# Attention over 128 blocks: the order of SyncE's waits ahead of the keys' transpose, and of the third unit's scores and maxima products

## The chip, the cores and the metric

The kernel runs on one core of a Trainium2 chip. The metric is the time of one execution on the device in microseconds (us), as the median of several runs. The core has TensorE (matrix products), VectorE, ScalarE, GpSimd and SyncE, each with its own queue of instructions, and 16 DMA engines. Engines meet at semaphores only: an instruction waits until a semaphore has reached a count, and all behind it on its queue wait with it.

## The reference

An audio tower of three stages over x of 128 blocks, 256 time steps, 192 channels: a tokenizer that turns 256 steps into 127 tokens, an attention with eight heads, and a feed-forward stage that picks one of four experts by token. The change is in the attention. Cut to it:

```python
def _L0_attn_ref(x, w_qkv, w_proj, b_proj):
    ...
    hd = C // H
    g = hd // 3
    scale = hd ** (-0.5)
    qkv = (x @ w_qkv.T).reshape(B, N, 3, H, hd).transpose(2, 0, 3, 1, 4)
    q, k, v = (qkv[0], qkv[1], qkv[2])
    q3, q4, q5 = (q[..., :g], q[..., g:2 * g], q[..., 2 * g:])
    k3, k4, k5 = (k[..., :g], k[..., g:2 * g], k[..., 2 * g:])
    v3, v4, v5 = (v[..., :g], v[..., g:2 * g], v[..., 2 * g:])
    ...
    x3 = merge(_attn(q4, jnp.concatenate([k3, k4], axis=2), jnp.concatenate([v3, v4], axis=2), scale))
    x4 = merge(_attn(q5, jnp.concatenate([k3, k5], axis=2), jnp.concatenate([v3, v5], axis=2), scale))
    x5 = merge(_attn(q5, jnp.concatenate([k4, k5], axis=2), jnp.concatenate([v4, v5], axis=2), scale))
    out = jnp.concatenate([x3, x4, x5], axis=2)
    return out @ w_proj.T + b_proj

h = h + _L0_attn_ref(_layernorm(h, axis=-1), L0_attn_w_qkv, L0_attn_w_proj, L0_attn_b_proj)
```

B is 128 blocks, N 127 tokens, C 192, H 8 heads of 24 channels, g 8.

## The kernel before

Four stages follow one another: `tokenize`, `norm_terms` (the layer norm's terms of all blocks), `attend`, and, after terms again, `feed_forward`. Only `attend` is touched.

`attend` is a pipeline over the 128 blocks, written out by hand. Each engine has a function `body(i, r)` that is run for i from -4 to 130 (r = i mod 4 picks ring buffers); the middle iterations stand in a hardware loop of four bodies, so that one pass of the loop is four blocks and ends with a branch. In iteration i, different engines work at different blocks:

- GpSimd normalises block i + 4 into `hx` (L818 to L826), splits `raw` into fp16 halves: the keys of block i + 3 (L801, L804, signal `pool_k`), its queries (L807, L810, signal `pool_q`; L812, signal `pool_q5`), and splits the finished `att` (L833, L835, signal `pool_y`).
- SyncE issues five DMA transposes between buffers of the core, each of which TensorE needs as an operand: `xt` of block i + 3 (L534), keys `kt` (L539) and queries `qt` (L544) of block i + 2, `yt` of block i - 2 (L549) and `qm`, the queries with their maxima in them, of block i + 1 (L555). Its helper `ready(signal, count)` waits for a signal and then raises a semaphore of SyncE's own (L527); where the count depends on the loop's register, a register instruction (L526) stands in the queue as well.
- TensorE runs `products(i, r, u)` for the four units u = 0 to 3, called first to fourth unit here. A unit makes the scores of two heads of block i (L583, `qm` by `kt`): `p_s1` in two halves, `p_s5` in two, `p_s0` in two; and, of a later block, the products of which VectorE takes the maxima (L587, `qt` by `kt`): two into `p_maxa` and two into `p_maxb`. The first two units work at the maxima products of block i + 1, the last two at those of block i + 2, so the third unit (u = 2) is the first that needs a block's `kt` and `qt` (semaphores `dma_k`, `dma_q`). All these matmuls use 24 or 32 of the array's 128 rows, named by j in the code: b, c, d, a are rows of four different groups, and `fourth` and `fifth` share theirs with c and d. Between the units stand the outputs (L653, probabilities by values), behind the third one qkv's product of block i + 3 (L620 to L626, into `p_z`) and a transpose (L664), behind the fourth the projection (L620 to L626 again, into `p_z`).
- ScalarE takes exponentials of the units' scores, L696 of `p_s1`, L700 of `p_s5`, L703 of `p_s0`; behind those of the third unit it copies qkv's product to `raw` (L721) and `vn` (L722).
- VectorE takes the maxima, L746 of `p_maxa` (signals `dve_ma`), L750 of `p_maxb` (`dve_mb`); behind the second unit's it puts the minima of two into the queries (L766, L767, signal `dve_min`).

`qt` has two buffers. Before SyncE writes one, it waits for the second unit's maxima products of the block that used it, `pe_ma[1]` and `pe_mb[1]`, which TensorE raises one iteration earlier. `kt` has four; before writing one it waits for the fourth unit's scores of block i - 2, `pe_s0[3]`.

Of the kernel before, what the change touches and what calls it, by code (L numbers as in the profile page):

```python
# [30 lines left out]
def seen(count):  # L31

    return max(count, 0) if isinstance(count, int) else count


def within(x, n):

    return not isinstance(x, int) or 0 <= x < n
# [412 lines left out]
def attend(nc, t, NB):  # L451

    with ExitStack() as ctx:
# [3 lines left out]
        U = 4  # L457
        NQ, NK = 3 * HEADS, 3 * HEADS
        K0 = NQ * 32
# [8 lines left out]
        qk = sb("qk", [128, 2, K0 + NK * 32], F16)  # L468
        vn = sb("vn", [128, U, 3 * HEADS * 32])
        kt = sb("kt", [128, U, 3, GRP, 128], F16)  # L470
# [8 lines left out]
        p_ma = ps("p_maxa", [128, 8, 128])  # L479
        p_mb = ps("p_maxb", [128, 4, 128])  # L480
        p_s = [ps("p_s0", [128, 4, 128]), ps("p_s1", [128, 4, 128])]
        p_s5 = ps("p_s5", [128, 4, 128])
# [10 lines left out]
        pool_khigh, pool_k, pool_qhigh, pool_q, pool_q5 = (sem(n) for n in ("pool_khigh", "pool_k", "pool_qhigh", "pool_q", "pool_q5"))  # L493
        dma_x, dma_k, dma_q, dma_y, dma_qm = (sem(n) for n in ("dma_x", "dma_k", "dma_q", "dma_y", "dma_qm"))
        pe_qkv, act_qk, act_v = sem("pe_qkv"), sem("act_qk"), sem("act_v")
        pe_ma = [sem(f"pe_ma{u}") for u in range(4)]
        pe_mb = [sem(f"pe_mb{u}") for u in range(4)]
        dve_ma = [sem(f"dve_ma{u}") for u in range(4)]
        dve_mb = [sem(f"dve_mb{u}") for u in range(4)]
        dve_min = sem("dve_min")  # L500
        pe_half = [sem(f"pe_half{u}") for u in range(4)]
        pe_s1 = [sem(f"pe_s1{u}") for u in range(4)]
        pe_s0 = [sem(f"pe_s0{u}") for u in range(4)]
        act_e5, act_e1, act_e0 = ([sem(f"act_e{n}{u}") for u in range(4)] for n in (5, 1, 0))
# [5 lines left out]
        def loop(eng, body):  # L510

            for i in range(-4, 3):
                body(i, i % U)
            rounds = (NB - 7) // U
            with eng.Fori(0, rounds) as j:
                for r in range(U):
                    body(j * U + (3 + r), (3 + r) % U)
            for i in range(3 + U * rounds, NB + 3):
                body(i, i % U)

        @block.sync
        def _(sp):

            def ready(signal, count):

                sp.wait_ge(signal, count)  # L526
                sp.sem_inc(sp_ready, 1)  # L527

            def body(i, r):
                if within(i + 3, NB):  # L530
                    ready(pool_x, seen(i + 4))
                    if within(i + 2, NB):
                        ready(pe_qkv, seen(i + 3))
                    sp.dma_start_transpose(xt[:, :, :], hx[:, (r + 1) % 2, :]).then_inc(dma_x, 16)  # L534
                if within(i + 2, NB):
                    ready(pool_k, seen(i + 3))
                    if within(i - 2, NB):
                        ready(pe_s0[3], seen(i - 1))
                    sp.dma_start_transpose(kt[:, (r + 2) % U].rearrange("p k g n -> p (k g) n"), qk[:, r % 2, K0:K0 + 768]).then_inc(dma_k, 16)  # L539
                    ready(pool_q, seen(i + 3))  # L540
                    if within(i, NB):
                        ready(pe_ma[1], seen(2 * (i + 1)))
                        ready(pe_mb[1], seen(i + 1))
                    sp.dma_start_transpose(qt[:, r % 2].rearrange("p k g n -> p (k g) n"), qk[:, r % 2, 0:512]).then_inc(dma_q, 16)  # L544
                if within(i - 2, NB):
                    ready(pool_y, seen(i - 1))
                    if within(i - 3, NB):
                        ready(pe_proj, seen(i - 2))
                    sp.dma_start_transpose(yt[:, :, :], ay[:, :]).then_inc(dma_y, 16)  # L549
                if within(i + 1, NB):  # L550
                    ready(dve_min, seen(i + 2))
                    ready(pool_q5, seen(i + 2))
                    if within(i - 1, NB):
                        ready(pe_s0[3], seen(i))
                    sp.dma_start_transpose(qm[:, (r + 1) % 2].rearrange("p v g n -> p (v g) n"), qk[:, (r + 1) % 2, 0:768]).then_inc(dma_qm, 16)  # L555
            loop(sp, body)

        def z_reader(i, use):
# [10 lines left out]
        def _(pe):  # L569
# [3 lines left out]
            def products(i, r, u):  # L573

                g, lo = u // 2, 2 * (u % 2)
                ahead, gm = (1, 1) if u < 2 else (2, 0)
                bm, rk, rq = i + ahead, (r + ahead) % U, (r + ahead) % 2
                a, b, c, d = lo, lo + 1, 2 - lo, 3 - lo
                fourth, fifth = (c, d) if u < 2 else (d, c)
                has_s, has_m = within(i, NB), within(bm, NB)  # L580

                def score(o, j, kind, versions, half=g):
                    return nc.tensor.matmul(o, kt[full(j), r, kind, half, :], qm[full(j), r % 2, versions, half, :],  # L583
                                            start=True, stop=True, skip_group_check=True)

                def maximum(o, j, kind, cols, half=gm):
                    return nc.tensor.matmul(o, qt[short(j), rq, kind, half, :], kt[short(j), rk, cols, half, :],  # L587
                                            start=True, stop=True, skip_group_check=True)

                if has_s:  # L590
                    if u == 0:
                        pe.wait_ge(dma_qm, seen(16 * (i + 1)))
                    pe.wait_ge(act_e1[u - 1] if u else act_e1[3], seen(i + 1 if u else i))
                    score(p_s[1][:, 0:2, :], b, 0, slice(0, 2))
                if has_m:
                    if u == 2:
                        pe.wait_ge(dma_k, seen(16 * (bm + 1)))
                        pe.wait_ge(dma_q, seen(16 * (bm + 1)))
                    pe.wait_ge(dve_ma[u - 1], seen(i + 2 if u < 3 else i + 3))
                    maximum(p_ma[:, 0:3, :], c, 1, slice(0, 3)).then_inc(pe_ma[u], 1)  # L600
                    maximum(p_ma[:, 4:7, :], d, 1, slice(0, 3)).then_inc(pe_ma[u], 1)
                if has_s:
                    score(p_s[1][:, 2:4, :], b, 1, slice(0, 3, 2)).then_inc(pe_s1[u], 1)
                if has_s:
                    pe.wait_ge(act_e5[u - 1] if u else act_e5[3], seen(i + 1 if u else i))
                    score(p_s5[:, 0:2, :], fifth, 2, slice(1, 3), 0)
                    score(p_s5[:, 2:4, :], fifth, 2, slice(1, 3), 1).then_inc(pe_half[u], 1)
                if has_s:
                    pe.wait_ge(act_e0[u - 1] if u else act_e0[3], seen(i + 1 if u else i))
                    score(p_s[0][:, 0:2, :], a, 0, slice(0, 2))  # L610
                    score(p_s[0][:, 2:4, :], a, 1, slice(0, 3, 2)).then_inc(pe_s0[u], 1)
                if has_m:
                    pe.wait_ge(dve_mb[u - 1], seen(i + 2 if u < 3 else i + 3))
                    maximum(p_mb[:, 0:2, :], fourth, 0, slice(0, 2), 0)
                    maximum(p_mb[:, 2:4, :], fourth, 0, slice(0, 2), 1).then_inc(pe_mb[u], 1)
# [51 lines left out]
            def body(i, r):  # L667
                before = (r - 1) % U
                if isinstance(i, int) and i == -2:
                    pe.wait_ge(consts, 3)  # L670

                products(i, r, 0)
                outputs(i - 1, before, 0, 2)
                outputs(i - 1, before, 1, 0)

                products(i, r, 1)
                outputs(i - 1, before, 1, 1)
                outputs(i - 1, before, 1, 2)

                products(i, r, 2)  # L680
                qkv(i)
                outputs_t(i)

                products(i, r, 3)
                proj(i)
                outputs(i, r, 0, 0)
                outputs(i, r, 0, 1)
# [522 lines left out]
```

## Time and profile before

| | us |
|---|---|
| median of 3 runs | 1877.03 (1873.08 to 1880.6) |
| the profiled execution | 1871.97 |
| its span, first to last instruction | 1870.2 |

| engine | busy us | share of the span |
|---|---|---|
| TensorE, matmuls | 1749.2 | 94% |
| TensorE, weight loads (beside matmuls) | 1016.4 | 54% |
| VectorE | 1498.9 | 80% |
| ScalarE | 1444.0 | 77% |
| GpSimd | 1251.8 | 67% |

Busy time is the time in which an engine has an instruction under way. Matmuls overlap each other, so a TensorE that is shown busy isn't at its peak. In a timeline a line is one instruction, or several of one source line in a row (x4), from the first start to the last end; "idle before" in brackets is the time in which the engine had nothing under way and what ended it, "issue" if nothing that the profile shows did. Waits of a queue itself, SyncE's signals and TensorE's semaphore instructions among them, have no lines of their own there and are seen as gaps. The attention stage runs from about 345 to 1400 us of the span.

### The profile page before, as it was taken

The numbers are of one execution on the slowest core, as the hardware profiler recorded it, in microseconds if no ns is written. First come the engines' busy times: TensorE is split into PE (matmuls) and PEld (weight loads), VectorE is DVE, ScalarE is ACT, GpSimd is POOL, SyncE is SP. The second block draws the span as 40 slices with busy tenths as digits, with TensorE's granted clock in tenths as the row PEclk, the third lists the DMA queues.
The fourth block names the chain that finished last, engine by engine and source line by source line (L and its number), as shares of the span: only waits on it lengthen the run. The fifth ranks groups of instructions, "written<-read, shape, count | busy, mean of one in ns | idle before, by whom it ended". The sixth has DMA issues, their size and how long they took to land. (4 is left out here: it accounts for less than half of the span.)

```text
span 1870.2 us, 56704 instructions
## 1 busy us (share of the span) xinstructions
PE 1749.2 (94%) x19008; PEld 1016.4 (54%) x19008; DVE 1498.9 (80%) x3546; ACT 1444.0 (77%) x2983; POOL 1251.8 (67%) x2306
## 2 busy tenths in 40 slices
PE   5999999589999999999999999999994999999999
PEld 3677777144444444444444444444442777777776
DVE  6877778589999999999999999999984555555554
ACT  4666666288888888888888888888884777777775
POOL 5777776477777777777777777777753565656661
PEclk9999999599999999999999999999997999999999
DMA  7344442154444444444444444444441333333332
GB/s 192 95 111 111 111 111 67 39 83 89 86 90 89 89 87 90 89 89 87 89 90 88 89 89 90 88 89 89 89 76 28 71 69 69 70 67 70 67 74 54
DMA packets 503935, 159.49 MB, mean 85 GB/s; under 512 B 452176, under 2 KB 503120, under 8 KB 503888
## 3 DMA queue, kind: packets, MB, share of 16 engines
q1 hardware_dynamic: 503888, 158.90, 40.1%
q8 instruction: 26, 0.43, 0.1%
q14 instruction: 21, 0.17, 0.0%
HBM read 37.26 MB, written 12.48 MB: 27 GB/s over the span
## 5 line engine op out<-in xcount | busy, mean ns | idle before, releaser
L746 DVE TENSOR_REDUCE tops<-p_maxa 128x6 f32<-128x762 f32 x512 | 483.7, 945 | 50.5 <-PE p_maxa L587 38.9
L653 PE MATMUL p_o<-probs,vn 127*32 127x256 f32 x6144 | 410.7, 385 | 0.4 <-DVE att L776 0.4
L696 ACT ACTIVATE probs<-p_s 128x512 f32<-128x512 f32 x512 | 306.3, 598 | 126.6 <-PE p_s L583 126.3
L583 PE MATMUL p_s<-qm,kt 32*128 32x256 f16 x3072 | 369.9, 272 | 3.3
L750 DVE TENSOR_REDUCE tops<-p_maxb 128x4 f32<-128x508 f32 x512 | 346.6, 677 | 0.0
L703 ACT ACTIVATE probs<-p_s 128x512 f32<-128x512 f32 x512 | 310.9, 607 | 0.0
L700 ACT ACTIVATE probs<-p_s 128x512 f32<-128x512 f32 x512 | 304.0, 594 | 0.0
L1055 DVE TENSOR_TENSOR gel_lo<-gel,gel_hi 128x512 f16<-128x512 f32 x192 | 151.2, 788 | 168.1 <-ACT gel_hi L1027 168.1
L583 PEld LDWEIGHTS p_s<-qm,kt 32*128 32x128 f16 x3072 | 149.3, 92 | 229.3 <-issue 126.4
L801 POOL TENSOR_TENSOR qk<-raw,one 128x384 f16<-128x384 f32 x128 | 105.7, 826 | 228.2 <-ACT raw L721 228.2
L653 PEld LDWEIGHTS p_o<-probs,vn 127*32 127x32 f32 x6144 | 160.5, 109 | 140.6 <-issue 74.4
L1019 ACT ACTIVATE gel<-f_w,b 128x512 f32<-128x512 f32 x192 | 131.9, 687 | 117.4 <-PE f_w L968 117.4
L587 PE MATMUL p_maxa<-kt,qt 24*128 24x384 f16 x1024 | 173.4, 333 | 37.3 <-issue 18.8
L587 PE MATMUL p_maxb<-kt,qt 24*128 24x256 f16 x1024 | 196.5, 272 | 0.2
L979 PE MATMUL f_y<-w_hi,gel_hi 128*128 128x192 f16 x768 | 188.8, 246 | 0.2 <-DVE gel_lo L1055 0.2
L981 PE MATMUL f_y<-w_hi,gel_lo 128*128 128x192 f16 x768 | 188.9, 246 | 0.0
L980 PE MATMUL f_y<-w_lo,gel_hi 128*128 128x192 f16 x768 | 188.8, 246 | 0.0
L1125 POOL TENSOR_TENSOR f_hx<-f_hn,f_one 128x192 f16<-128x192 f32 x120 | 85.5, 712 | 153.7 <-ACT f_hn L1006 151.0
L208 ACT ACTIVATE tanhs<-pa 128x384 f32<-128x384 f32 x128 | 62.7, 490 | 99.2 <-PE pa L154 99.2
L1027 ACT ACTIVATE gel_hi<-gel 128x512 f16<-128x512 f32 x192 | 120.9, 630 | 7.0
L396 POOL TENSOR_TENSOR diag<-ident,weight 128x256 f32<-128x256 f32 x128 | 79.2, 620 | 54.1 <-DVE weight L296 44.9
L183 PE MATMUL ph<-zs,band 128*128 128x192 f32 x512 | 105.4, 330 | 3.1 <-DVE band L317 2.2
(212 smaller groups left out, 4509.9 us busy)
## 6 DMA issues: line engine op xcount, KB each, us to landing
xt_a<-in_xt SPq DMA_DIRECT2D x32, 512.0 KB, 4.4
xt_b<-in_xt SPq DMA_DIRECT2D x64, 256.0 KB, 5.1
out<-out_sb SPq DMA_DIRECT2D x32, 336.0 KB, 2.6
xt<-hx SPq DMA_TRANSPOSE x128, 2.4
kt<-qk SPq DMA_TRANSPOSE x128, 2.8
qt<-qk SPq DMA_TRANSPOSE x128, 2.4
qm<-qk SPq DMA_TRANSPOSE x128, 2.7
yt<-ay SPq DMA_TRANSPOSE x128, 2.3
```

What stands on the lines that cost most here:

```text
L583: return nc.tensor.matmul(o, kt[full(j), r, kind, half, :], qm[full(j), r % 2, versions, half, :], start=True, stop=True, skip_group_check ...
L587: return nc.tensor.matmul(o, qt[short(j), rq, kind, half, :], kt[short(j), rk, cols, half, :], start=True, stop=True, skip_group_check=True)
L653: last = nc.tensor.matmul(p_o[32 * j:32 * j + 32, blocks, :], vn[0:NP, r, src:src + 32], probs[0:NP, r % 2, QUAD * g + j, kind * 256:(kind ...
L696: nc.scalar.activation(probs[:, r % 2, h + 1, 0:512], p_s[1][:, :, :].rearrange("p x n -> p (x n)"), ACT.Exp, scale=SCALE).then_inc(act_e1 ...
L700: nc.scalar.activation(probs[:, r % 2, fifth:HEADS:QUAD, 512:768], p_s5[:, :, :].rearrange("p (h x) n -> p h (x n)", h=2), ACT.Exp, scale= ...
L703: nc.scalar.activation(probs[:, r % 2, h, 0:512], p_s[0][:, :, :].rearrange("p x n -> p (x n)"), ACT.Exp, scale=SCALE).then_inc(act_e0[u], 1)
L746: nc.vector.tensor_reduce(top[:, q, 6 * pair:6 * pair + 6].rearrange("p (e k) -> p e k", e=2), p_ma[:, :, :].rearrange("p (e k) n -> p e k ...
L750: nc.vector.tensor_reduce(top[:, q, 24 + 4 * fourth:28 + 4 * fourth], p_mb[:, :, 0:NP], AX.X, ALU.max, negate=True)\
L979: nc.tensor.matmul(o, ghi[:, c % 3, n], t.w2_hi[:, c, :], start=False, stop=False)
L980: nc.tensor.matmul(o, ghi[:, c % 3, n], t.w2_lo[:, c, :], start=False, stop=False)
L981: last = nc.tensor.matmul(o, glo[:, c % 3, n], t.w2_hi[:, c, :], start=False, stop=(c == HCH - 1))
L1055: nc.vector.tensor_tensor(glo[:, c % 3, :], gel[:, c % 2, :], ghi[:, c % 3, :], ALU.subtract).then_inc(dve_lo[c], 1)
```

## The change

SyncE: in the part of its body for block i + 2, the waits `pe_ma[1]`, `pe_mb[1]` (which stood between `kt`'s and `qt`'s transposes) and `pe_s0[3]` (which stood between the wait for `pool_k` and `kt`'s transpose) now stand ahead of the wait for `pool_k`. TensorE: two pieces of a unit become functions, `large` (the wait for `kt` and `qt` and the two products into `p_maxa`) and `odd` (the second half of `p_s1` and both of `p_s5`); the units 0, 1 and 3 run them in the order they had, the third unit runs `odd` first.

```diff
--- before.py
+++ after.py
@@ -533,14 +533,14 @@
                         ready(pe_qkv, seen(i + 3))
                     sp.dma_start_transpose(xt[:, :, :], hx[:, (r + 1) % 2, :]).then_inc(dma_x, 16)
                 if within(i + 2, NB):
-                    ready(pool_k, seen(i + 3))
-                    if within(i - 2, NB):
-                        ready(pe_s0[3], seen(i - 1))
-                    sp.dma_start_transpose(kt[:, (r + 2) % U].rearrange("p k g n -> p (k g) n"), qk[:, r % 2, K0:K0 + 768]).then_inc(dma_k, 16)
-                    ready(pool_q, seen(i + 3))
                     if within(i, NB):
                         ready(pe_ma[1], seen(2 * (i + 1)))
                         ready(pe_mb[1], seen(i + 1))
+                    if within(i - 2, NB):
+                        ready(pe_s0[3], seen(i - 1))
+                    ready(pool_k, seen(i + 3))
+                    sp.dma_start_transpose(kt[:, (r + 2) % U].rearrange("p k g n -> p (k g) n"), qk[:, r % 2, K0:K0 + 768]).then_inc(dma_k, 16)
+                    ready(pool_q, seen(i + 3))
                     sp.dma_start_transpose(qt[:, r % 2].rearrange("p k g n -> p (k g) n"), qk[:, r % 2, 0:512]).then_inc(dma_q, 16)
                 if within(i - 2, NB):
                     ready(pool_y, seen(i - 1))
@@ -587,24 +587,35 @@
                     return nc.tensor.matmul(o, qt[short(j), rq, kind, half, :], kt[short(j), rk, cols, half, :],
                                             start=True, stop=True, skip_group_check=True)
 
+                def large(do):
+
+                    if do:
+                        if u == 2:
+                            pe.wait_ge(dma_k, seen(16 * (bm + 1)))
+                            pe.wait_ge(dma_q, seen(16 * (bm + 1)))
+                        pe.wait_ge(dve_ma[u - 1], seen(i + 2 if u < 3 else i + 3))
+                        maximum(p_ma[:, 0:3, :], c, 1, slice(0, 3)).then_inc(pe_ma[u], 1)
+                        maximum(p_ma[:, 4:7, :], d, 1, slice(0, 3)).then_inc(pe_ma[u], 1)
+
+                def odd(do):
+
+                    if do:
+                        score(p_s[1][:, 2:4, :], b, 1, slice(0, 3, 2)).then_inc(pe_s1[u], 1)
+                        pe.wait_ge(act_e5[u - 1] if u else act_e5[3], seen(i + 1 if u else i))
+                        score(p_s5[:, 0:2, :], fifth, 2, slice(1, 3), 0)
+                        score(p_s5[:, 2:4, :], fifth, 2, slice(1, 3), 1).then_inc(pe_half[u], 1)
+
                 if has_s:
                     if u == 0:
                         pe.wait_ge(dma_qm, seen(16 * (i + 1)))
                     pe.wait_ge(act_e1[u - 1] if u else act_e1[3], seen(i + 1 if u else i))
                     score(p_s[1][:, 0:2, :], b, 0, slice(0, 2))
-                if has_m:
-                    if u == 2:
-                        pe.wait_ge(dma_k, seen(16 * (bm + 1)))
-                        pe.wait_ge(dma_q, seen(16 * (bm + 1)))
-                    pe.wait_ge(dve_ma[u - 1], seen(i + 2 if u < 3 else i + 3))
-                    maximum(p_ma[:, 0:3, :], c, 1, slice(0, 3)).then_inc(pe_ma[u], 1)
-                    maximum(p_ma[:, 4:7, :], d, 1, slice(0, 3)).then_inc(pe_ma[u], 1)
-                if has_s:
-                    score(p_s[1][:, 2:4, :], b, 1, slice(0, 3, 2)).then_inc(pe_s1[u], 1)
-                if has_s:
-                    pe.wait_ge(act_e5[u - 1] if u else act_e5[3], seen(i + 1 if u else i))
-                    score(p_s5[:, 0:2, :], fifth, 2, slice(1, 3), 0)
-                    score(p_s5[:, 2:4, :], fifth, 2, slice(1, 3), 1).then_inc(pe_half[u], 1)
+                if u == 2:
+                    odd(has_s)
+                    large(has_m)
+                else:
+                    large(has_m)
+                    odd(has_s)
                 if has_s:
                     pe.wait_ge(act_e0[u - 1] if u else act_e0[3], seen(i + 1 if u else i))
                     score(p_s[0][:, 0:2, :], a, 0, slice(0, 2))
```

TensorE's queue, the third unit in the first body of the hardware loop, before, from the first half of `p_s1` to the register instruction ahead of qkv's product (`act_e11`, `act_e51`, `act_e01` are ScalarE's signals that the second unit's scores are read, `dve_ma1`, `dve_mb1` VectorE's for its maxima):

```order
L583 MATMUL p_s1<-qm,kt 128x256 [waits act_e11]
L597 ISA
L587 MATMUL p_maxa<-kt,qt 128x384 [waits dve_ma1,dma_q,dma_k]
L587 MATMUL p_maxa<-kt,qt 128x384
L583 MATMUL p_s1<-qm,kt 128x256
L583 MATMUL p_s5<-qm,kt 128x256 [waits act_e51]
L583 MATMUL p_s5<-qm,kt 128x256
L583 MATMUL p_s0<-qm,kt 128x256 [waits act_e01]
L583 MATMUL p_s0<-qm,kt 128x256
L587 MATMUL p_maxb<-kt,qt 128x256 [waits dve_mb1]
L587 MATMUL p_maxb<-kt,qt 128x256
L630 ISA
```

And with the change:

```order
L583 MATMUL p_s1<-qm,kt 128x256 [waits act_e11]
L583 MATMUL p_s1<-qm,kt 128x256
L583 MATMUL p_s5<-qm,kt 128x256 [waits act_e51]
L583 MATMUL p_s5<-qm,kt 128x256
L594 ISA
L587 MATMUL p_maxa<-kt,qt 128x384 [waits dve_ma1,dma_q,dma_k]
L587 MATMUL p_maxa<-kt,qt 128x384
L583 MATMUL p_s0<-qm,kt 128x256 [waits act_e01]
L583 MATMUL p_s0<-qm,kt 128x256
L587 MATMUL p_maxb<-kt,qt 128x256 [waits dve_mb1]
L587 MATMUL p_maxb<-kt,qt 128x256
L641 ISA
```

The three scores (second half of `p_s1`, both of `p_s5`) went from behind the two products into `p_maxa`, which carry the waits for `dma_q` and `dma_k`, to ahead of them; L594 and L597 are the register instruction for these counts.

SyncE's queue, a later body of the hardware loop, before, from the register instruction ahead of `xt` to `qm`:

```order
L526 REGISTER_ALU
L534 DMA_TRANSPOSE xt<-hx 128x3x128 [waits pool_x,pe_qkv]
L539 DMA_TRANSPOSE kt<-qk 128x6x128 [waits pool_k,pe_s03]
L526 REGISTER_ALU [waits pool_q]
L544 DMA_TRANSPOSE qt<-qk 128x4x128 [waits pe_ma1,pe_mb1]
L549 DMA_TRANSPOSE yt<-ay 128x3x128 [waits pool_y,pe_proj]
L555 DMA_TRANSPOSE qm<-qk 128x6x128 [waits dve_min,pool_q5,pe_s03]
```

And with the change:

```order
L526 REGISTER_ALU
L534 DMA_TRANSPOSE xt<-hx 128x3x128 [waits pool_x,pe_qkv]
L526 REGISTER_ALU
L542 DMA_TRANSPOSE kt<-qk 128x6x128 [waits pe_ma1,pe_mb1,pe_s03,pool_k]
L544 DMA_TRANSPOSE qt<-qk 128x4x128 [waits pool_q]
L549 DMA_TRANSPOSE yt<-ay 128x3x128 [waits pool_y,pe_proj]
L555 DMA_TRANSPOSE qm<-qk 128x6x128 [waits dve_min,pool_q5,pe_s03]
```

`pe_ma[1]`, `pe_mb[1]` and the register instruction went from between `kt` and `qt` to ahead of `kt`, and `pool_k` is now the last that `kt` waits for.

## Rows read from the trace of the kernel before

**Rows 1.** The page: the span of the profiled execution and its instructions.
```profile
span 1870.2 us, 56704 instructions
```

**Rows 2.** Busy times of a stretch: engines, then TensorE's granted clock, DMA share, GB/s.
```profile
900.00:1000.00 100.00, 96.03 (x1259) 45.90 (x1252) 94.20 (x174) 88.35 (x186) 74.35 (x151) 1.00 0.45 89
```

**Rows 3.** Groups of 500 to 1400 us: busy us, mean ns, idle before them and its end.
```profile
L696 ACT ACTIVATE probs<-p_s 128x512 f32<-128x512 f32 x442 | 264.4, 598 | 107.1 <-PE p_s L583 107.0
...
L587 PE MATMUL p_maxa<-kt,qt 24*128 24x384 f16 x884 | 148.3, 330 | 20.4 <-issue 15.0 <-DMA kt<-qk 2.6
```

**Rows 4.** Timeline of SyncE's queue: start us, length us, queue, line, transfer.
```profile
911.19 1.21 SPq L555 DMA_TRANSPOSE qm<-qk  x1
913.09 1.18 SPq L534 DMA_TRANSPOSE xt<-hx  x1
914.75 1.21 SPq L539 DMA_TRANSPOSE kt<-qk  x1
...
919.38 1.21 SPq L555 DMA_TRANSPOSE qm<-qk  x1
920.85 1.18 SPq L534 DMA_TRANSPOSE xt<-hx  x1
922.93 1.21 SPq L539 DMA_TRANSPOSE kt<-qk  x1
924.46 1.19 SPq L544 DMA_TRANSPOSE qt<-qk  x1
...
927.55 1.21 SPq L555 DMA_TRANSPOSE qm<-qk  x1
...
947.25 1.21 SPq L539 DMA_TRANSPOSE kt<-qk  x1
```

**Rows 5.** The page's DMA issues (KB, us to landing), and the answer on the tile qt.
```profile
qt<-qk SPq DMA_TRANSPOSE x128, 2.4
...
DMA to landing us min/median/max: 2.4/2.4/2.4
```

**Rows 6.** Timeline of TensorE's matmuls over one block (rows at one source line are merged).
```profile
917.14 0.27 PE L587 MATMUL p_maxb<-kt,qt 24*128 24x256 f16 x1
...
919.30 0.39 PE L620 MATMUL p_z<-wqkv_ahi,xt 128*128 128x512 f16 x1
...
920.18 0.38 PE L626 MATMUL p_z<-wqkv_chi,xt 128*128 128x512 f16 x1
...
923.10 0.28 PE L583 MATMUL p_s<-qm,kt 32*128 32x256 f16 x1
...
923.12 0.39 PE L583 MATMUL p_s<-qm,kt 32*128 32x256 f16 x3
...
923.59 1.07 PE L653 MATMUL p_o<-probs,vn 127*32 127x256 f32 x16
...
926.50 0.28 PE L583 MATMUL p_s<-qm,kt 32*128 32x256 f16 x1
926.97 0.34 PE L587 MATMUL p_maxa<-kt,qt 24*128 24x384 f16 x2 [0.20 <-issue]
...
927.46 0.39 PE L620 MATMUL p_z<-wqkv_ahi,xt 128*128 128x512 f16 x1
```

**Rows 7.** Timeline of ScalarE, the same block.
```profile
919.24 0.60 ACT L696 ACTIVATE probs<-p_s 128x512 f32<-128x512 f32 x1 [0.27 <-PE p_s L583]
...
920.69 0.46 ACT L721 ACTIVATE raw<-p_z 128x320 f32<-128x320 f32 x1
```

**Rows 8.** Timeline of GpSimd, the same block.
```profile
922.21 0.55 POOL L804 TENSOR_TENSOR qk<-raw,qk 128x192 f16<-128x192 f32 x1
...
923.41 0.43 POOL L810 TENSOR_TENSOR qk<-raw,qk 128x128 f16<-128x128 f32 x1
```

**Rows 9.** Timeline of VectorE, the same block.
```profile
925.24 0.94 DVE L746 TENSOR_REDUCE tops<-p_maxa 128x6 f32<-128x762 f32 x1
...
927.11 0.22 DVE L767 TENSOR_TENSOR qk<-tops 128x16 f16<-128x16 f32 x1
```

## The prediction

> **What bounds the kernel now.** I first read the page and the busy times of a stretch of the attention stage, which the change touches alone. There TensorE is busy 96% at a granted clock of 1.00 [rows 1, 2]; that share says no more than that little can wait. Next come the groups of 500 to 1400 us: the reader is to see that TensorE's idle time of its matmuls stands almost only before `p_maxa` (20.4 us) and ScalarE's before the exponential of L696 (107.1 us) [rows 3]. Then the timelines of one block, which tell why.
>
> Take the block from 919.30 to 927.46, the starts of two first products of `p_z` [rows 6]. Four blocks take 947.25 - 914.75 = 32.50 us, so 8.125 each on the mean [rows 4]; this one takes 8.16.
>
> - ScalarE copies `raw` at 920.69 [rows 7]. GpSimd makes the keys' halves, ending at 922.21 + 0.55 = 922.76, and the queries' last half that counts here by 923.41 + 0.43 = 923.84 [rows 8].
> - SyncE issues the keys' transpose (kt) at 922.93, 0.17 behind the keys. That instruction holds it for 1.21, to 924.14. The queries' transpose (qt) goes at 924.46, 0.32 later, though the queries had been ready since 923.84 [rows 4, 8].
> - qt takes 2.4 us to land, least, median and most [rows 5]: 926.86. TensorE begins the third unit (u = 2) at 926.50 with one score and stands at `p_maxa` until 926.97 [rows 6]. A unit that waits for nothing takes 923.59 - 923.10 = 0.49 us (the first unit); this one takes 0.96.
> - Behind `p_maxa` stand `p_s1`'s second half and so ScalarE's exponential, which waits 0.27 us [rows 7], and qkv's product, 0.49 behind `p_maxa`, from which the next `raw` comes.
>
> This is a closed loop: raw to `p_maxa` 926.97 - 920.69 = 6.28, `p_maxa` to qkv 0.49, qkv to raw 920.69 - 919.30 = 1.39; sum 8.16, the block's whole length. No engine's work bounds the block; this loop through SyncE's queue does.
>
> **The change part by part.**
>
> *SyncE's waits.* Nothing is added: three signals (`pe_ma[1]`, `pe_mb[1]`, `pe_s0[3]`) and the register instruction for one of them move ahead of the wait for `pool_k`. What does one cost? From the end of one transpose to the next issue, qm to xt takes 920.85 - 919.38 - 1.21 = 0.26 with two signals and a register instruction, kt to qt 0.32 with three signals and one [rows 4]. So an instruction is about 0.06 to 0.07. Behind `pool_k`, `pe_s0[3]` goes: kt comes 0.07 earlier against the keys. Between kt and qt two signals and the register instruction go: 3 x 0.07 = 0.20 of 0.32. Together 0.27 off the loop, if SyncE has idle time ahead of `pool_k` for them. It has: xt ends at 922.03 and kt starts at 922.93, 0.90 later, of which two signals need 0.2; in the block with the loop's branch 914.75 - 913.09 - 1.18 = 0.48, of which the same 0.2 and now 0.27 more with the three signals and the register instruction just fit [rows 4]. The moved work costs nothing as long as that cover lasts (see the next limit). qt's landing is taken as unchanged, 2.4. The bounds for this part: 0.27 if the landing follows the issue, 0 if the transfer starts behind something else that the rows don't show.
>
> *The scores ahead of the maxima products* (unit 2 alone). Same matmuls, same count. Three scores no longer stand behind the wait for qt: `p_s1`'s second half, and with it the exponential of L696. That one started at 919.24 and waited 0.27 [rows 7]; now it would follow ScalarE's own work, 0.27 earlier. So ScalarE no longer sets the start of raw; next late is the end of qkv's product, 920.18 + 0.38 = 920.56 [rows 6], and with 0.05 for the signal (an estimate, half of the 0.11 between qt's landing and `p_maxa`) raw starts at 920.61 instead of 920.69: 0.08 off the loop. It can't cost through L696, which gets its input no later than it did. Do the maxima come later? They use other rows of the array than `b`, and the fifth head's two scores share rows with the first maxima product. In the first unit `p_s` x3 starts at 923.12, 0.02 behind the unit's first [rows 6]; the second score of the same rows can't be among them yet, so a later one of free rows is: matmuls of free rows don't wait for earlier ones of busy rows. The stretch behind qt's landing then stays 0.49.
>
> The Trainium skill says otherwise ("TensorE: Matmul & The Clock Gate", section Part 3, packing small matmuls): matmuls start and end in strict program order. By it the maxima would stand behind the two fifth-head scores, some 0.22 us into the unit; with the unit starting at 926.50 that is still no later than qt's landing with 0.27 off, within 0.1. The row speaks against the rule, and the sum would be smaller by 0.05 a block at most.
>
> Loop with both parts: 6.28 - 0.27 + 0.49 + 1.39 - 0.08 = 7.81 in this block, 0.35 less; on the mean 8.125 - 0.35 = 7.775.
>
> **What is late next.** TensorE's own loop: raw to the third unit 926.50 - 920.69 = 5.81, a unit 0.49, qkv to raw 1.31: 7.61, not late [rows 6, 7]. SyncE's own: VectorE's L767 ends at 927.11 + 0.22 = 927.33, and qm is issued 0.22 later, at 927.55 [rows 4, 9]. qm to xt 1.47, and 913.09 - 911.19 = 1.90 in the block with the branch. xt to kt in the new order: 1.18 + 0.32 + one signal 0.07 = 1.57. kt to qt 1.21 + 0.12 = 1.33. qt to `p_maxa` 926.97 - 924.46 = 2.51, then 0.49 and 1.31 to raw; raw to the end of L767 927.33 - 920.69 = 6.64. The sum is 0.22 + 1.47 + 1.57 + 1.33 + 2.51 + 0.49 + 1.31 + 6.64 = 15.54 for two blocks, 7.77 each: level with the first loop. With the branch 15.97 (1.90 for 1.47). One loop pass is four blocks: 15.97 + 15.54 = 31.51, or 7.88 a block. So the pre-waits lose their cover just in the branch's block, and the mean falls by 8.125 - 7.88 = 0.245 to 0.26 (between the roundings of the rows). I take 0.255.
>
> *The sum.* 128 blocks [rows 5], of which the first few fill the pipeline: 122 x 0.255 = 31 us. Fill, drain and the other stages stay. The profiled execution took 1871.97 us (span 1870.2 [rows 1]); with the change 1841. The median of the runs is 1877.03, 5.06 above that execution; I apply the gain to it: **1846 us**.
>
> **The rivals.**
> 1. *The queries' loop alone bounds.* For it: SyncE may make up for the branch in the three other blocks, whose cover was 0.90. Against: the two loops are level, so there is little to make up. Gain 0.35 x 124 = 43: 1834.
> 2. *Half a change.* qt's landing doesn't follow its issue, or the moved waits lose their cover in all blocks; then 0.08 for the scores stays, and up to 0.10 of SyncE's 0.27. For it: kt and qt now follow one another 0.20 closer on one queue. Against: of all qt's in the stretch of rows 5 the least and the most took the same 2.4, though kt stood 1.53 or 1.57 us before them [rows 4]. Gain 10 to 22: 1855 to 1867.
> 3. *It doesn't do what it says*: the wait at `p_maxa` is not qt's but another's (VectorE's, say). Against: 924.46 + 2.4 ends 0.11 ahead of `p_maxa` [rows 4 to 6], and VectorE's maximum, whose buffer it needs, was done at 925.24 + 0.94 = 926.18 [rows 9]. Gain 0: 1877.
> 4. *Slower.* The signals of the second unit now stand ahead of kt. If SyncE had to wait there, kt and all behind it (qt, yt, qm, xt) would be held, and TensorE at `p_maxa` behind them. The count asked for is that of the second unit one iteration back, done at 917.14 + 0.27 = 917.41 [rows 6]; SyncE asks from 922.03 and needs it by 922.76. It decides only if that signal came more than 922.76 - 917.41 = 5.3 us later than it does. Were it that of the same iteration, which comes up to 926.50, kt would go 3.6 us later and each block take as much more: 122 x 3.6, 2316 us.
>
> **How the numbers follow.** Forecast 0.56, rival 1 0.20, rival 2 0.14, rival 3 0.07, rival 4 0.03. The range leaves out rivals 3 and 4 and the upper half of 2: low is rival 1 with 3 us for rounding, 1831; high is the gain of rival 2's middle, 1860. What a measurement tells from no change here is about 0.5%, 9 us, so faster means below 1867.6: forecast, rival 1 and nearly all of rival 2, 0.89; same 0.08; slower 0.03.
>
> **What would show it.** In the changed kernel's timelines: kt to qt 1.33 instead of 1.53 to 1.60; kt 0.1 behind the keys' halves in three blocks of four and later in the one with the branch; the third unit 0.65 long in three blocks of four and longer in the one with the branch; no idle time ahead of L696 in the third unit; raw 1.31 behind qkv's first product; four kt's 31.5 us apart. The SyncE step is wrong if qt's landing takes over 2.5; the scores' step is wrong if VectorE's maximum of the third unit starts later against qkv than it did and waits for `p_maxa`; the limit is wrong if the branch's block is as short as the others.

## The result

| | us |
|---|---|
| before, median of 4 runs | 1875.56 (1873.08 to 1880.6) |
| changed kernel, median of 4 runs | 1846.91 (1843.65 to 1848.77) |
| ratio, 95% interval | 0.9842 (0.9816 to 0.9868) |
| span of the profiled execution, before and after | 1870.2 and 1844.7 |

In the changed kernel the exponential of `p_s1` stands at L707, L732 copies `raw`, and qkv's first product is L631. The stretch that answers to [rows 2], with the same columns:

```profile
900.00:1000.00 100.00, 98.00 (x1297) 47.61 (x1290) 95.39 (x178) 90.21 (x190) 76.39 (x154) 1.00 0.46 92
```

TensorE's busy share went from 96.03 to 98.00 at the same granted clock of 1.00. The groups that answer to [rows 3]:

```profile
L707 ACT ACTIVATE probs<-p_s 128x512 f32<-128x512 f32 x447 | 266.4, 596 | 72.7 <-PE p_s L583 72.6
...
L587 PE MATMUL p_maxa<-kt,qt 24*128 24x384 f16 x880 | 151.2, 331 | 8.2 <-issue 8.0 <-DVE tops L757 0.2
```

ScalarE's idle time ahead of `p_s1`'s exponential fell from 107.1 to 72.7 us, TensorE's ahead of `p_maxa` from 20.4 to 8.2. SyncE's queue, as [rows 4]:

```profile
906.18 1.18 SPq L534 DMA_TRANSPOSE xt<-hx  x1
908.22 1.21 SPq L542 DMA_TRANSPOSE kt<-qk  x1
909.55 1.20 SPq L544 DMA_TRANSPOSE qt<-qk  x1
...
912.92 1.21 SPq L555 DMA_TRANSPOSE qm<-qk  x1
914.39 1.18 SPq L534 DMA_TRANSPOSE xt<-hx  x1
915.96 1.21 SPq L542 DMA_TRANSPOSE kt<-qk  x1
917.28 1.20 SPq L544 DMA_TRANSPOSE qt<-qk  x1
...
923.71 1.21 SPq L542 DMA_TRANSPOSE kt<-qk  x1
...
928.39 1.21 SPq L555 DMA_TRANSPOSE qm<-qk  x1
930.30 1.19 SPq L534 DMA_TRANSPOSE xt<-hx  x1
931.99 1.21 SPq L542 DMA_TRANSPOSE kt<-qk  x1
...
939.84 1.21 SPq L542 DMA_TRANSPOSE kt<-qk  x1
```

Four blocks take 939.84 - 908.22 = 31.62 us, 7.905 each, where they took 8.125. From the end of kt to the issue of qt it is now 909.55 - 908.22 - 1.21 = 0.12, where it was 0.32. From kt to kt three blocks take 7.74, 7.75 and 7.85 and the one between 923.71 and 931.99, in which SyncE's queue has the loop's branch (qm to xt 930.30 - 928.39 = 1.91 instead of 1.47), takes 8.28. One block of TensorE, ScalarE and GpSimd, as [rows 6 to 8]:

```profile
911.86 0.39 PE L583 MATMUL p_s<-qm,kt 32*128 32x256 f16 x4
912.08 0.33 PE L587 MATMUL p_maxa<-kt,qt 24*128 24x384 f16 x1
912.08 0.28 PE L583 MATMUL p_s<-qm,kt 32*128 32x256 f16 x1
912.10 0.32 PE L587 MATMUL p_maxa<-kt,qt 24*128 24x384 f16 x1
...
912.56 0.39 PE L631 MATMUL p_z<-wqkv_ahi,xt 128*128 128x512 f16 x1
...
913.43 0.38 PE L637 MATMUL p_z<-wqkv_chi,xt 128*128 128x512 f16 x1
```

```profile
912.00 0.49 ACT L723 ACTIVATE ot<-p_o 128x384 f32<-128x384 f32 x1
912.38 0.59 ACT L707 ACTIVATE probs<-p_s 128x512 f32<-128x512 f32 x1
...
913.85 0.44 ACT L732 ACTIVATE raw<-p_z 128x320 f32<-128x320 f32 x1
```

```profile
907.58 0.55 POOL L815 TENSOR_TENSOR qk<-raw,qk 128x192 f16<-128x192 f32 x1
```

and qt's landing in the same form as in [rows 5], of the five transposes of qt from 905 to 945 us:

```profile
DMA to landing us min/median/max: 2.4/2.4/2.4
```

The third unit takes 912.56 - 911.86 = 0.70 instead of 0.96: four scores start together with the unit, the products into `p_maxa` 0.22 behind it, 0.13 behind qt's landing at 909.55 + 2.4 = 911.95. The exponential at 912.38 follows ScalarE's own copy of `ot` without a wait; before it waited 0.27. `raw` starts 913.85 - 912.56 = 1.29 behind qkv's first product (1.39 before). The keys end at 907.58 + 0.55 = 908.13 and kt goes at 908.22, 0.09 later (0.17 before).

The block with the branch, whose kt goes at 931.99, looks different (GpSimd, TensorE, ScalarE):

```profile
930.82 0.55 POOL L815 TENSOR_TENSOR qk<-raw,qk 128x192 f16<-128x192 f32 x1
```

```profile
935.19 0.39 PE L583 MATMUL p_s<-qm,kt 32*128 32x256 f16 x4
935.83 0.34 PE L587 MATMUL p_maxa<-kt,qt 24*128 24x384 f16 x2 [0.25 <-issue]
...
936.32 0.39 PE L631 MATMUL p_z<-wqkv_ahi,xt 128*128 128x512 f16 x1
```

```profile
937.69 0.44 ACT L732 ACTIVATE raw<-p_z 128x320 f32<-128x320 f32 x1 [0.41 <-PE p_z L637]
```

Its keys end at 930.82 + 0.55 = 931.37, so here SyncE is 0.62 behind them and not 0.09: it is the queue that is late. The third unit takes 936.32 - 935.19 = 1.13, and `raw` starts 1.37 behind qkv's first product, hardly less than before the change.

### The profile page after: what moved, and what is told of

The parts are those of the page before. It is cut to its first block and busy times, and to the rows that moved or that the text cites. A ratio compares the mean times of both kernels' runs of the same rounds, so it can differ in the third digit from the quotient of the medians.

```text
span 1844.7 us, 56704 instructions
## 1 busy us (share of the span) xinstructions
PE 1747.4 (95%) x19008; PEld 1021.8 (55%) x19008; DVE 1486.3 (81%) x3546; ACT 1443.1 (78%) x2983; POOL 1250.6 (68%) x2306
## 5 line engine op out<-in xcount | busy, mean ns | idle before, releaser
L707 ACT ACTIVATE probs<-p_s 128x512 f32<-128x512 f32 x512 | 305.2, 596 | 84.1 <-PE p_s L583 83.7
L583 PE MATMUL p_s<-qm,kt 32*128 32x256 f16 x3072 | 349.5, 273 | 4.1 <-DMA qm<-qk 1.1
L583 PEld LDWEIGHTS p_s<-qm,kt 32*128 32x128 f16 x3072 | 135.4, 93 | 227.2 <-issue 126.7
L587 PE MATMUL p_maxa<-kt,qt 24*128 24x384 f16 x1024 | 177.5, 334 | 21.9 <-issue 10.6
```

Source lines behind the costliest of these rows:

```text
L707: nc.scalar.activation(probs[:, r % 2, h + 1, 0:512], p_s[1][:, :, :].rearrange("p x n -> p (x n)"), ACT.Exp, scale=SCALE).then_inc(act_e1 ...
```

## Experiments

The theory is that of the prediction: two closed loops run through SyncE's queue. The queries' loop (raw, GpSimd's halves, kt, qt, third unit, qkv, raw) bounded the kernel before; the change shortens it to about 7.78 a block; then SyncE's own loop (`dve_min`, qm, xt, kt, qt, third unit, ..., `dve_min`, over two blocks) is level, and where the hardware loop's branch stands in it, late. The rivals are that only one part does the work, that an engine's work is the limit, and that the long block is not SyncE's. All ratios are to the kernel before on the same chip, run beside it, and the length of a block is the mean between kt's rows of four or eight blocks from about 900 us on.

**One part alone.** SyncE's waits as in the change, the units all in the old order:

```diff
-                if u == 2:
-                    odd(has_s)
-                    large(has_m)
-                else:
-                    large(has_m)
-                    odd(has_s)
+                large(has_m)
+                odd(has_s)
```

> SyncE's part alone; the third unit stands as before, with the second half of p_s1 behind the wait for qt. Theory (two loops through SyncE's queue): the queries' loop falls by 0.27 to 7.86 a block; ScalarE's exponential still waits for TensorE, so raw stays 1.38 behind qkv's first product; SyncE's own loop with the branch gives 15.62 + 16.05 for four blocks, 7.92. Gain over the kernel before 0.20 x 122 = 25 us, ratio 0.987. Rival (the scores' order does the work, qt's landing does not follow its issue): ratio 1.00.

Measured 1851.74 us, ratio 0.9881 (0.986 to 0.9902); kt's 896.42 to 928.20, 7.945 a block (7.92 expected). The interval holds the theory's 0.987. Its remark that ScalarE's exponential of `p_s1` still waits is true of the branch's block alone, where it stands idle 0.37 us; in the three others it follows ScalarE's own copy of `ot` within 0.01, and `raw` starts 1.35 to 1.38 behind qkv's product all the same.

And the new order of the third unit alone, with SyncE's waits where they were:

```diff
-                    if within(i, NB):
-                        ready(pe_ma[1], seen(2 * (i + 1)))
-                        ready(pe_mb[1], seen(i + 1))
-                    if within(i - 2, NB):
-                        ready(pe_s0[3], seen(i - 1))
                     ready(pool_k, seen(i + 3))
+                    if within(i - 2, NB):
+                        ready(pe_s0[3], seen(i - 1))
                     sp.dma_start_transpose(kt ...)
                     ready(pool_q, seen(i + 3))
+                    if within(i, NB):
+                        ready(pe_ma[1], seen(2 * (i + 1)))
+                        ready(pe_mb[1], seen(i + 1))
                     sp.dma_start_transpose(qt ...)
```

> The third unit's new order alone; SyncE's waits as before. Theory: only the 0.08 between ScalarE's and qkv's end goes, 8.125 to 8.04 a block, 10 us, ratio 0.995; the third unit stays 0.9 long, since qt still lands as late. Rival (the scores' order does most): ratio 0.985 to 0.99.

Measured 1863.7 us, ratio 0.9941 (0.9919 to 0.9964); kt's 893.54 to 925.67, 8.03 a block, where 8.04 was expected. TensorE's timeline in the third unit:

```profile
913.16 0.39 PE L583 MATMUL p_s<-qm,kt 32*128 32x256 f16 x4
913.64 0.34 PE L587 MATMUL p_maxa<-kt,qt 24*128 24x384 f16 x2
...
914.13 0.39 PE L631 MATMUL p_z<-wqkv_ahi,xt 128*128 128x512 f16 x1
```

The unit is 914.13 - 913.16 = 0.97 long, as before the change: the four scores run and then TensorE stands for qt all the same. So the order gives its 0.09 a block not through the unit but through ScalarE: no idle time is left ahead of its exponential, and `raw` starts 1.29 behind qkv's first product in three blocks of four (1.38 in all four before). Both parts together (8.125 - 7.905 = 0.22) give less than the sum of each alone (0.18 + 0.09), which fits a second limit that comes in as the first loop shortens.

**Which of the three scores.** In the changed kernel the two scores of `p_s5` go back behind the maxima products of the third unit; only `p_s1`'s second half stays ahead:

```diff
                     if do:
-                        score(p_s[1][:, 2:4, :], b, 1, slice(0, 3, 2)).then_inc(pe_s1[u], 1)
+                        if u != 2:
+                            score(p_s[1][:, 2:4, :], b, 1, slice(0, 3, 2)).then_inc(pe_s1[u], 1)
...
-                if u == 2:
-                    odd(has_s)
-                    large(has_m)
-                else:
-                    large(has_m)
-                    odd(has_s)
+                if u == 2 and has_s:
+                    score(p_s[1][:, 2:4, :], b, 1, slice(0, 3, 2)).then_inc(pe_s1[u], 1)
+                large(has_m)
+                odd(has_s)
```

> The changed kernel, but in the third unit only the second half of p_s1 stands ahead of the maxima products; the two scores of p_s5 stand behind them as before. Theory: what the new order gives comes from ScalarE's exponential of p_s1 alone; the scores of p_s5 are needed 0.49 us later than p_s1's, and the stretch behind qt's landing is as long: 7.88 to 7.90 a block, ratio 0.984. Rival (the fifth head's scores count: they fill the wait for qt and would lengthen the stretch behind it by up to 0.1 now): 7.95 or more, ratio 0.987 to 0.990.

Measured 1846.35 us, ratio 0.9858 (0.9837 to 0.9879); kt's 892.44 to 924.06, 7.905 a block, the changed kernel's own length. No part of the fifth head's scores is seen.

**The dose of SyncE's signals.** Three more waits for a signal long given between kt and qt of the changed kernel:

```diff
+                    for _ in range(3):
+                        ready(pool_k, seen(i + 3))
                     ready(pool_q, seen(i + 3))
                     sp.dma_start_transpose(qt ...)
```

> The changed kernel with three more waits for a signal long given between kt and qt (0.07 each, 0.20 together), which puts back what stood there. Theory: the queries' loop 7.98, the four blocks with the branch 15.97 + 0.20 + 2 x 7.98 = 32.13, 8.03 a block; 16 us slower than the changed kernel, ratio to before 0.993. Rival (qt's issue does not matter): ratio 0.984.

Measured 1865.72 us, ratio 0.996 (0.9943 to 0.9977); kt's 891.76 to 923.97, 8.05 a block (8.03 expected). 0.2 us on a queue that computes nothing costs most of the gain. In time it cost more than expected: 0.993 lies outside the interval. The profiled execution, from which the block's length is read, was the fastest of nine with 1859.7 us; what the others spent beyond it no trace shows.

The same three ahead of the wait for the keys, where the change put its own:

```diff
+                    for _ in range(3):
+                        ready(pool_x, seen(i + 3))
                     ready(pool_k, seen(i + 3))
                     sp.dma_start_transpose(kt ...)
```

> The changed kernel with three more waits for a signal long given, ahead of the wait for the keys (pool_k), where the change put its own. Theory (the cover there is used up in the branch's block): SyncE's own loop grows by 0.20 per two blocks, four blocks 16.17 + 15.75 = 31.92, 7.98 a block, 9 us slower than the changed kernel, ratio to before 0.989. Rival (there is idle time enough): 0.984.

Measured 1859.47 us, ratio 0.9935 (0.9919 to 0.995), where 0.989 was expected: the direction is the theory's and the cost about half as much again. SyncE's queue in it:

```profile
906.47 1.21 SPq L544 DMA_TRANSPOSE kt<-qk  x1
...
914.31 1.21 SPq L544 DMA_TRANSPOSE kt<-qk  x1
...
922.42 1.22 SPq L544 DMA_TRANSPOSE kt<-qk  x1
...
930.13 1.21 SPq L544 DMA_TRANSPOSE kt<-qk  x1
...
936.74 1.18 SPq L534 DMA_TRANSPOSE xt<-hx  x1
938.61 1.21 SPq L544 DMA_TRANSPOSE kt<-qk  x1
```

Four blocks take 32.14 us, 8.035 each (7.98 expected). The lengths are 7.84, 8.11, 7.71 and 8.48: the branch's block, and the one two blocks away from it, are long, the others between them are not. A loop that closes over two blocks fits that; a fixed amount of an engine's work in each block would lengthen all four alike. The cover ahead of the keys is used up in these two. Of the 0.22 us over four blocks beyond the expected 31.92, 0.12 is a register instruction that the sum left out (see the part on the prediction); the other 0.10 stays open.

**The branch.** First, eight bodies instead of four in a pass of the hardware loop of all engines:

```diff
-            rounds = (NB - 7) // U
+            rounds = (NB - 7) // (2 * U)
             with eng.Fori(0, rounds) as j:
-                for r in range(U):
-                    body(j * U + (3 + r), (3 + r) % U)
-            for i in range(3 + U * rounds, NB + 3):
+                for r in range(2 * U):
+                    body(j * (2 * U) + (3 + r), (3 + r) % U)
+            for i in range(3 + 2 * U * rounds, NB + 3):
                 body(i, i % U)
```

> The changed kernel with eight bodies of the attention in one pass of the hardware loop instead of four, so half as many branches. Theory (the branch on SyncE's queue takes back what the queries' loop would give): the block with the branch was 8.26 long where the others were 7.73 to 7.86; with one in eight the mean falls from 7.90 to 7.84, 8 us faster than the changed kernel, ratio to before 0.980. Rival (the block's length is set by an engine's work, and the long block is a shift between blocks): same as the changed kernel, 0.984.

Measured 1950.34 us, ratio 1.0409 (1.0381 to 1.0436). Neither theory. In the middle of the stage one block in eight took 11 to 13.6 us, one in each pass and not in every second, and the others 7.7 to 9.2. The page's row of the instruction queue (packets, MB, share), in this run and in the changed kernel:

```profile
q8 instruction: 155, 2.54, 0.6%
```

```profile
q8 instruction: 26, 0.43, 0.1%
```

155 packets of instructions instead of 26. In the changed kernel none falls between 418 and 1342 us of the span; here they go on all through the attention. So it looks as if the doubled body were fetched anew in each pass, where the body of four stayed in place; no run takes the fetching away and shows it as the cause. The run says nothing on SyncE's branch. So the doubled body went to SyncE's loop alone (`loop(sp, body, 2 * U)`, with the pass length as an argument; all others keep four):

> The changed kernel with eight bodies in a pass of SyncE's hardware loop alone; all other engines keep four. With eight bodies on every engine the instruction transfers rose from 26 to 155 and every second pass a block took 11 to 13 us, so that run told nothing of SyncE's branch. Theory (the branch on SyncE's queue makes the long block): one block in eight is 8.2 long, the mean falls from 7.90 to 7.84, 8 us faster than the changed kernel, ratio to before 0.980. Rival (another engine's branch or work makes it): still one in four, 0.984.

Measured 1835.82 us, ratio 0.9813 (0.9796 to 0.9829). Kt's rows:

```profile
894.87 1.21 SPq L542 DMA_TRANSPOSE kt<-qk  x1
...
941.60 1.21 SPq L542 DMA_TRANSPOSE kt<-qk  x1
...
949.32 1.21 SPq L542 DMA_TRANSPOSE kt<-qk  x1
...
957.62 1.21 SPq L542 DMA_TRANSPOSE kt<-qk  x1
```

Eight blocks take 957.62 - 894.87 = 62.75, 7.844 each, as expected to 0.01; one of them is 957.62 - 949.32 = 8.30 long, the other seven 7.72 to 7.89. The long block moved with SyncE's branch alone, from one in four to one in eight. The same on the kernel before:

> The kernel before with eight bodies in a pass of SyncE's loop alone. Theory: there SyncE had 0.2 to 0.9 us of idle time ahead of the keys even in the branch's block, so nothing changes, ratio 1.00 within 0.002. Rival (SyncE's branch always costs): 0.995 or less.

Measured 1871.11 us, ratio 0.9995 (0.9983 to 1.0006); kt's 888.80 to 953.71, 8.114 a block. Before the change the branch cost next to nothing: the queries' loop covered it.

**Without the signals.** What `pe_ma[1]`, `pe_mb[1]` and `pe_s0[3]` ask for, TensorE finished ahead of the qkv product from which `pool_k` comes (or, for qm, ahead of the maxima from which `dve_min` comes): in [rows 6] the second unit's maxima products end at 917.41 and qkv's last product of the same iteration at 920.56. The changed kernel without these waits:

```diff
-                    if within(i, NB):
-                        ready(pe_ma[1], seen(2 * (i + 1)))
-                        ready(pe_mb[1], seen(i + 1))
-                    if within(i - 2, NB):
-                        ready(pe_s0[3], seen(i - 1))
                     ready(pool_k, seen(i + 3))
...
                     ready(pool_q5, seen(i + 2))
-                    if within(i - 1, NB):
-                        ready(pe_s0[3], seen(i))
                     sp.dma_start_transpose(qm ...)
```

> The changed kernel without the waits for pe_ma[1], pe_mb[1] and pe_s0[3] on SyncE's queue, ahead of kt and ahead of qm; what they ask for is implied by what pool_k and dve_min ask for, since TensorE finished it earlier in its own order. Theory: SyncE's own loop loses four signals and a register instruction, 0.34 per two blocks, 15.20 and 15.63 with the branch; then the queries' loop, 7.78, is the limit: 7.79 a block, 14 us faster than the changed kernel, ratio to before 0.977. Rival (the queries' loop is not at 7.78 but where the changed kernel is, 7.90): 0.984.

Measured 1831.45 us, ratio 0.9777 (0.9763 to 0.9792). SyncE's queue and a stretch's busy times:

```profile
905.53 1.21 SPq L537 DMA_TRANSPOSE kt<-qk  x1
...
936.66 1.21 SPq L537 DMA_TRANSPOSE kt<-qk  x1
```

```profile
900.00:1000.00 100.00, 98.81 (x1313) 49.03 (x1316) 96.69 (x181) 91.31 (x193) 76.98 (x155) 1.00 0.46 92
```

Four blocks take 31.13, 7.783 each: the length that the queries' loop alone was forecast to have, 7.775. In its block with the branch, qm to xt is 1.79 and not 1.91, so a little more than the signals has gone from SyncE's loop. With eight bodies on SyncE's loop as well:

> The changed kernel without the implied waits and with eight bodies in a pass of SyncE's loop. Theory: without the waits SyncE's own loop is no longer late even with the branch (all four blocks of a pass took 7.72 to 7.86), so the branch costs nothing now: same as the run without the waits, 7.78 a block, ratio 0.978. Rival (the two gains add): 7.72, ratio 0.973.

Measured 1835.69 us, ratio 0.9794 (0.9775 to 0.9813); kt's 895.35 to 957.77, eight blocks, 7.80 each. The two don't add: once SyncE's own loop is short enough, the branch is covered again.

The changed kernel and the one without the signals on one chip:

> The changed kernel itself, beside the next run on one chip, since their ratios so far come from different calls. Expected: 7.90 a block, ratio to before 0.984 to 0.986.

> The kernel without the implied waits again, on the same chip as the changed kernel. Theory: 7.78 a block, 0.12 x 117 = 14 us less than the changed kernel, intervals apart, ratio to before 0.977. Rival (the difference between calls was the chip's): the two within 3 us of each other.

Measured 1845.15 us, ratio 0.9858 (0.9843 to 0.9874), and 1830.89 us, ratio 0.9786 (0.9772 to 0.9799). They are 14.3 us apart, where 14 was expected, and the intervals don't touch. The kernel without the implied waits beats both.

## Why the prediction was right, and where it was off

It forecast 1846 us and 1846.91 was measured. So near a hit is partly chance; by its steps:

- *What bounds the kernel.* Right. The loop through SyncE's queue was named, and each experiment that put time on this queue or took it off gave the block's length that was forecast within 0.06 us (the one with eight bodies on all engines measured something else). In whole time the two with three more signals cost more than forecast, 0.996 for 0.993 and 0.9935 for 0.989.
- *SyncE's part, 0.27 a block.* Right: kt 0.08 nearer to the keys, qt 0.20 nearer to kt, the landing 2.4 as before although the two transfers stand closer.
- *The scores' part, 0.08.* Right in three blocks of four, and through the reason given: `raw` starts 1.29 to 1.31 behind qkv's product, 1.31 was forecast. In the branch's block it starts 1.37 behind, so there the part gives 0.01. Alone it gave 0.09; on top of SyncE's part it gave 7.945 - 7.905 = 0.04.
- *The rule against it* (the Trainium skill, "TensorE: Matmul & The Clock Gate", section Part 3, has matmuls start and end in strict program order). For the starts this case's trace disagrees: in the first unit of the kernel before, at 923.10, the first product into `p_s0`, seventh in program order, starts at 923.12, ahead of the fourth at 923.22. For the ends it agrees with the page. The lengths in the rows are modelled, but the semaphore events are not, and in that unit they come in program order: 923.45 and 923.48 (`p_maxa`), 923.52 (`p_s1`), 923.67 (`p_s5`), 923.71 (`p_s0`), 923.76 (`p_maxb`). They do so in all first and third units from 500 to 1330 us of the kernel before, the changed one and the one with one score. So a product that starts early doesn't signal early. The changed kernel's maxima at 0.22 into the unit can't decide between the two readings, since qt's landing frees them at the same time. Moving two scores ahead of the maxima or back leaves a block at 7.905, so nothing of the sum hung on the rule.
- *What is late next.* Right in kind. Kt goes 0.09 to 0.13 behind the keys in three blocks of four and 0.62 in the branch's, and the third unit is 0.64 to 0.70 long in the three and 1.13 in that one, as forecast. It holds the largest mis-sized term. Forecast 31.51 / 4 = 7.88 a block, a gain of 0.2475, taken as 0.255 without a reason; measured 7.905. The step is "xt to kt in the new order: 1.57": in the branch's block, which the sum needs, it is 931.99 - 930.30 = 1.69. The gap behind xt was put together from one with three signals and one register instruction; in the trace the first body of the loop has four signals and two register instructions there and the third body four and one, and so 0.12 more. Over four blocks 31.51 + 0.12 = 31.63, against 31.62 in the trace. That this comes out to the hundredth is partly chance: `raw` in the branch's block is 0.06 later than the 1.31 of the sum, and in the other round the stretch from `raw` to the end of the minima takes 6.56 instead of 6.64.
- *The sum, 122 blocks.* The steady stretch is shorter at its gain: from the ninth kt to the third last it is 117 block lengths, from 418.13 to 1369.78 us before and from 416.63 to 1342.42 now, 951.65 and 925.79 us, so 25.9 us less. The last kt's of before and after:

```profile
1369.78 1.21 SPq L539 DMA_TRANSPOSE kt<-qk  x1
...
1388.29 1.21 SPq L539 DMA_TRANSPOSE kt<-qk  x1
```

```profile
1342.42 2.55 SPq L542 DMA_TRANSPOSE kt<-qk  x1
...
1362.95 1.21 SPq L542 DMA_TRANSPOSE kt<-qk  x1
```

  After the loop's exit the last two blocks take 1388.29 - 1369.78 = 18.5 us before and 20.5 now. Those 2 us belong to this one execution and not to the change: in the profile of the changed kernel's second run, on another chip, they take 18.6, and there the steady stretch fell by 26.0 and the span, 1841.6 us, by 28.6:

```profile
1341.24 2.42 SPq L542 DMA_TRANSPOSE kt<-qk  x1
...
1359.86 1.21 SPq L542 DMA_TRANSPOSE kt<-qk  x1
```

  So about 26 us of the gain stand in the steady stretch, and 1.5 to 2.5 us ahead of it, of which 0.7 to 1.5 us lie ahead of the first kt, where nothing was changed. The prediction forecast 31, 122 blocks of 0.255; the medians fell by 28.7. And it started from a median of 1877.03 that with one run more was 1875.56. The gain was 2.4 us too large and the start 1.5 too high, so more than half of the one error is hidden by the other.
- *The rivals.* The queries' loop alone as the limit (rival 1, 1834) is not this kernel but the one without the signals, 1831. Half a change, no change and slower didn't come.

## What to carry over

Where all engines are nearly full and none is the bound, look for the closed loop: add the steps from one event to the same event of the next block, and see whether they make up the block's length; waits of 0.07 us on a queue that only issues transfers count in full when the queue is in that loop. Put waits that are long fulfilled ahead of the wait that comes last, and better drop those which another wait implies; and when a loop is shortened, sum the next one, the rare branch in it included, over as many blocks as it takes to close.

## What the runs showed of the hardware

- A wait with its signal on SyncE costs about 0.07 us even when it has long been fulfilled: three more between kt and qt took the gap from 0.12 to 0.32 us. A register instruction costs about as much (0.12 in the branch's block, 1.69 against 1.57).
- The branch of the hardware loop adds 0.44 us on that queue (qm to xt 1.91 against 1.47). Two register instructions that stand there and not in the other bodies are in the 0.44. It isn't a constant: in the kernel without the implied waits, with the same instructions, it is 0.32 (1.79 against 1.47), and no run says why.
- Matmuls on different rows of the array can start out of program order, yet their signals come in program order (the first unit of the kernel before at 923.10: the seventh product starts at 923.12, the fourth at 923.22; the signal of the fourth comes at 923.52, of the eighth at 923.71).
- Doubling the body of the hardware loop on all engines raised the instruction packets from 26 to 155 and the time by 4.1% against before, where doubling SyncE's alone left the packets at 26 and made it faster. That fetching the bodies anew is the cause is read from the packets and not shown by a run that takes it away.
- A DMA transpose's landing, 2.4 us, didn't change when the one ahead of it was issued 0.2 us closer (1.33 instead of 1.53 us).
